# Splitting the first convolution load and moving the first low-rank second products in a two-layer convolution and low-rank FFN kernel

## What is computed

```
c0 = grouped_conv1d(x, weight, 9 taps, 4 groups) + cond @ c_weight.T + bias
x  = x + c0 @ W.T + b + mask * (c0 @ A.T) @ B.T          # low-rank adapters by batch entry
w  = softmax(mlp(cond));  c1 = (sum_k w_k W_k) @ x + sum_k w_k b_k
x  = x + 2 * sum_experts gate * (c1 @ A_e) @ B_e          # top 16 of 64 experts
```

## Time and profile before

| | |
|---|---|
| median of 3 runs | 661.34 us (660.93 to 661.41) |
| profiled execution | 659.91 us, its span 658.1 us |
| PE busy | 649.5 us (99% of the span) |
| VectorE, ScalarE, GpSimd busy | 451.2, 213.5, 72.9 us |
| memory traffic | 157.98 MB, 240 GB/s over the span |

### The profile page before, as it was taken

How to read it: one execution, slowest core, us unless ns; L and a number is a source line. 1 busy time by engine, 2 the same in 40 slices (tenths; PEclk the granted TensorE clock), 3 DMA queues, 4 the chain that set the end, 5 groups by cost and what they waited for, 6 DMA issues and landing times.

```text
span 658.1 us, 8354 instructions
## 1 busy us (share of the span) xinstructions
PE 649.5 (99%) x3197; PEld 537.6 (82%) x3197; DVE 451.2 (69%) x690; ACT 213.5 (32%) x275; POOL 72.9 (11%) x91
## 2 busy tenths in 40 slices
PE   9999999999999999999999999999999999999997
PEld 8878888888897788888789788888879888888875
DVE  2859469549378888558779648636867856665775
ACT  2714235315134024335124312334423421433420
POOL 1499300000000160000000042000000000000000
PEclk9999999999999999999999999999999999999999
DMA  8587714984988836776985682274987665037685
GB/s 314 196 292 279 296 49 135 356 247 167 392 280 346 336 149 255 272 225 251 366 296 186 266 319 96 101 225 161 366 323 268 259 252 190 0 116 206 223 333 215
DMA packets 51450, 157.98 MB, mean 240 GB/s; under 512 B 5472, under 2 KB 6368, under 8 KB 51424
## 3 DMA queue, kind: packets, MB, share of 16 engines
q1 hardware_dynamic: 46096, 148.05, 62.0%
q10 hardware_dynamic: 5328, 9.61, 4.8%
HBM read 131.94 MB, written 25.71 MB: 240 GB/s over the span
## 4 chain that ended last, share of the span: by engine, by line
PE 74%; DMA 12%; DVE 7%; issue 2%; ACT 2%; SPq 1%; ACTq 0%; DVEq 0%
PE bank L1367 19%; PE bank L1369 19%; PE bank L1368 19%; PE bank L1381 7%; DMA gate_x<-gates 5%; DMA piece_lo<-kept 4%; PE bank L1401 3%; DMA raw<-pieces 2%; PE bank L1388 2%; PE bank L1393 1%; PE bank L1407 1%; PE bank L1395 1%; DMA toep<-taps 1%; PE bank L1408 1%; DVE x L918 1%
## 5 line engine op out<-in xcount | busy, mean ns | idle before, releaser
L886 DVE TENSOR_TENSOR piece_lo<-raw,piece_hi 128x1024 fp32r<-128x1024 f32 x60 | 74.2, 1240 | 90.1 <-ACT piece_hi L639 89.8
L639 ACT ACTIVATE piece_hi<-raw 128x1024 fp32r<-128x1024 f32 x60 | 63.3, 1057 | 143.9 <-PE bank L1369 100.5
L1367 PE MATMUL bank<-piece_hi,u_hi 128*128 128x512 f32 x272 | 107.9, 397 | 0.1
L1369 PE MATMUL bank<-piece_hi,u_lo 128*128 128x512 f32 x272 | 107.3, 394 | 0.0
L1368 PE MATMUL bank<-piece_lo,u_hi 128*128 128x512 f32 x272 | 107.3, 394 | 0.0
L1367 PE MATMUL bank<-v_hi,piece_hi 128*128 128x512 f32 x256 | 101.8, 398 | 0.0
L1369 PE MATMUL bank<-v_hi,piece_lo 128*128 128x512 f32 x256 | 101.1, 395 | 0.0
L1368 PE MATMUL bank<-v_lo,piece_hi 128*128 128x512 f32 x256 | 101.0, 394 | 0.0
L1367 PE MATMUL bank<-piece_hi,v_hi 128*128 128x512 f32 x192 | 76.2, 397 | 1.1 <-DMA piece_lo<-kept 1.0
L1369 PE MATMUL bank<-piece_hi,v_lo 128*128 128x512 f32 x192 | 75.8, 395 | 0.0
L1368 PE MATMUL bank<-piece_lo,v_hi 128*128 128x512 f32 x192 | 75.8, 395 | 0.0
(11 more groups left out here) (143 smaller groups left out, 799.2 us busy)
## 6 DMA issues: line engine op xcount, KB each, us to landing
raw<-pieces SPq DMA_DIRECT2D x76, 512.0 KB, 5.3
piece_hi<-kept SPq DMA_DIRECT2D x48, 512.0 KB, 4.7
piece_lo<-kept SPq DMA_DIRECT2D x48, 512.0 KB, 6.1
conv_in<-conv_x SPq DMA_DIRECT2D x16, 516.0 KB, 6.8
x<-x SPq DMA_DIRECT2D x16, 512.0 KB, 5.4
gate_x<-gates ACTq DMA_DIRECT2D x32, 256.0 KB
out<-x SPq DMA_DIRECT2D x32, 256.0 KB, 4.4
conv_in<-pieces SPq DMA_DIRECT2D x12, 512.0 KB, 8.6
```

The source lines that it names most:

```text
L639: act.activation(piece_hi[:, n % SLOTS, :], raw[:, r % RAWS, :], ACT.Copy).then_inc(s_piece_hi, 1)
L886: dve.tensor_tensor(piece_lo[:, n % SLOTS, :], raw[:, r % RAWS, :], piece_hi[:, n % SLOTS, :].bitcast(F32), ALU.subtract).then_inc(s_piece ...
L1367: pe.matmul(to, left_hi, right_hi, start=first, stop=False)
L1369: return pe.matmul(to, left_lo, right_hi, start=False, stop=last)
```

## The change

The first load of convolution input brings entry 0 alone; entry 1's half follows behind taps 1 and taps 3, with a semaphore of its own, for which PE waits ahead of entry 1. In `ffn_piece`, the low-rank second products of the first half are issued behind all four tiles of piece 3, with their waits; those of the second half stay behind each tile of piece 7.

```diff
+        s_convin_b1 = sem("s_convin_b1")
...
-            load_conv_in(0, 0)
+            def load_first(b, done):
+                width = CG * (Q + 1)
+                sp.dma_start(conv_in[:, b].rearrange("p g q -> p (g q)"),
+                             conv_x[0, 0, :, b * width:(b + 1) * width]).then_inc(done, 16)
+
+            load_first(0, s_convin[0])
             load_taps(sp, 1)
             load_taps(sp, 3)
+            load_first(1, s_convin_b1)
             sp.dma_start(hidden_stage, hidden_w).then_inc(s_hidden_w, 16)
...
                         if t == NT - 1:
                             mm.then_inc(s_piece_used, 1)
-                        if j == 3:
-                            if t == 0:
-                                pe.wait_ge(s_lora_s, 2)
-                                pe.wait_ge(s_lora_lo, 1)
-                                if h == 0:
-                                    pe.wait_ge(s_const_hi, 3)
-                                    pe.wait_ge(s_const_lo, 2)
-                            lora_second(h, t, 4 * h + t, False)
+                        if n == 7:
+                            lora_second(1, t, 4 + t, False)
+                    if n == 3:
+                        pe.wait_ge(s_lora_s, 2)
+                        pe.wait_ge(s_lora_lo, 1)
+                        pe.wait_ge(s_const_hi, 3)
+                        pe.wait_ge(s_const_lo, 2)
+                        for t in range(NT):
+                            lora_second(0, t, t, False)
...
                     if b % 2 == 0:
                         pe.wait_ge(s_convin[b // 2], 16)
+                    elif b == 1:
+                        pe.wait_ge(s_convin_b1, 16)
```

## The result

| | before | after |
|---|---|---|
| median, 22 runs each | 660.51 us (658.61 to 662.91) | 658.83 us (657.23 to 661.17) |
| ratio after / before | | 0.9978, 95% interval 0.9968 to 0.9988 |
| profiled execution, its span | 659.91, 658.1 us | 658.74, 656.9 us |
| PE busy | 649.5 us | 649.5 us |

The ratio is 1.45 us of 660.51, with an interval from 0.8 to 2.1 us; the two medians are 1.68 us apart. The forecast of the difference, 1.5 us, was met.

The account below looks back on a forecast made before the run. TensorE (PE) was taken to set the pace, busy 649.5 of 658.1 us. The start's 0.35 us and the low-rank wait's 1.14 us sum to 1.49 us: 661.34 - 1.5 = 659.8 us, range 659.1 to 661.1.

Parts of the forecast that it names:

- The anchor: Starting time for the whole kernel: differences from the trace are subtracted from the runs' median of 661.34 us.
- Part 2: Low-rank second products behind all four tiles of piece 3: PE's wait there goes, 1.14 us, at least 0.9.
- the second copy: ScalarE copy before the low-rank second products: claimed to release PE at 48.51 us after 0.91 us without work.
- Part 1: Start of the kernel, first load halved: taps come earlier and PE starts 0.35 us sooner, bounds 0 and 0.45.
- the hidden weights: Weights of the first hidden product at the start: land at 8.32 us, against a use at 8.32, just in time.
- the wait of 0.42 us for taps: PE's wait before tap group 3 at the start, 0.23 to 0.42 us, taken as gone.
- Rival 1: Only the low-rank wait goes and the start stays as it is: 660.2 us, within 0.2%; chance 0.11.
- all engines are where they were, only earlier: From the second group's row-wise selection to the end, the chain moves by the same 1.5 us.
- The wait at 187.65 us: PE's first wait after 52 us, for VectorE, 0.47 us: appears near 186.2 with its size unchanged.
- 2: Rival: the second half's fixed cost is not overlapped, PE 1.25 us late on hidden weights: 661.4 us; chance 0.04.
- 3: Rival: the second half is stuck in the backlog, batch entry 1 is 4.2 us late: 664.4 us; chance 0.04.
- Rival 4: Gain taken back at the DMA-bound stretch, PE's wait at 187.65 us grows by 1 us: 660.9 us; chance 0.09.

Follow-up runs that it names:

- dose: Changed kernel with added products nobody reads: 24 gave ratio 1.0120 to the kernel before, 5 gave 1.0023 and 1.0030, 5 ahead of the mixing 1.0022.
- e11: Changed kernel with low-rank second products of tiles 0 and 1 behind tile 1, those of tiles 2 and 3 behind their own; ratio 0.9981 to the kernel before.
- e8: Changed kernel plus small fills by idle engines behind each tap group's landing; one execution, group 3 landed at 6.95 us.
- e7: Kernel before with the low-rank move alone, old load, plus small fills behind each tap group's landing; one execution, group 3 landed at 8.04 us.
- e2: Kernel before with only the low-rank second products moved, first load as before; ratio 0.9985 (0.9971 to 0.9999) to the kernel before.
- e6: The kernel before once more, unchanged; ratio 0.9999 (0.9984 to 1.0015).
- e1: Kernel before with only the first load split, low-rank products where they stood; ratio 1.0000 (0.9988 to 1.0013) to the kernel before.
- e12: The split load alone on the kernel before, a second time; ratio 1.0001 (0.9988 to 1.0013) to the kernel before.
- e10: The changed kernel once more, unchanged; ratio 0.9977 (0.9960 to 0.9993) to the kernel before.
- e16: The changed kernel a third time, unchanged; ratio 0.9982 (0.9970 to 0.9994) to the kernel before.
- e4: Changed kernel with 6 warm-up products in place of 12; median 660.75 us, ratio 1.0006 (0.9993 to 1.0019) to the kernel before.
- e3: Kernel before with 6 warm-up products in place of 12; median 661.93 us, ratio 1.0045 (1.0023 to 1.0066) to the kernel before.

## Why the prediction was right, and where it was not

**The anchor failed.** The step that put the time outside the range was "I take the differences from the trace and subtract them from the median", with 0.25 us for the spread of the runs. Three runs had given 661.34 us (660.93 to 661.41). 22 runs gave 660.51 us, from 658.61 to 662.91. The three lay 0.8 us above the median of the many, and their spread of 0.5 us stood for one of 4.3 us. Of the miss of 659.8 - 658.83 = 1.0 us, 0.8 is this, and the rest is 1.68 us between the medians in place of 1.5; no mechanism was wrong by as much. The range has a slip too: 659.7 less 0.25 is 659.45, and not 659.2.

**Part 2 was right in mechanism and size.** 1.14 us forecast, 1.16 measured in A, in the first profile after and in six more without a dose, always 35.35 us. One reading was wrong and cost nothing: it was VectorE's subtraction and not the second copy that released PE, and where that took 0.84 us the stall was 1.3 us, so that the close agreement is partly luck of the profile before. The waits moved behind 18 more products are covered with over 3 us to spare; e11 shows that six would do. GpSimd's start on the mixing weights was hidden as argued.

**Part 1 was right in mechanism and unproved in size.** The taps come sooner, group 3 by 0.36 us on average (1.08 in e8 against e7) where 0.58 was worked out, and the next late thing is the hidden weights, as the prediction put it, 8.4 us against 8.32. Over the eleven profiles with the split they landed at 8.25 to 8.85 us, so that they now and then held PE up themselves (0.20 us in e8). The first half is hidden by the warm-up. But the wait of 0.42 us for taps in the one profile was taken as the state of the kernel. It is one draw: in e2, with the old load, group 3 had landed at 7.49 us and the passes ran through with next to no wait (entry 1 at 8.63 us); in e6 the waits were longer (9.38). The 0.35 us is 0.24 us on average over 16 profiles, and by the times alone (e1, e12) anything from 0.9 us lost to 0.8 us gained. In the first profile after, the first weight piece started at 24.24 us where 23.9 was forecast and 24.26 measured before. Rival 1, that only the low-rank wait goes, cannot be told from the forecast by the whole kernel's time.

**The way to the end.** The prediction's 1:1 fits the change itself: 1.16 + 0.24 = 1.4 us against 1.45 (0.8 to 2.1) measured. The doses say that what is put in at 52 us can come out larger at the end. So the step "all engines are where they were, only earlier" is not a law of this kernel, and the good fit of the sum leaves room for both a smaller part 1 and a gain of more than 1:1. No single profile can decide it: from the mixing to PE's last product the twelve profiles without a dose took 574.3 to 576.4 us, whatever the kernel. That stays open. The wait at 187.65 us was taken for a fixed feature. It was missing in the first profile after, in e10 and in the unchanged kernel's second profile e6, and there again in e16 (0.3 and 0.4 us): it comes and goes without any change. It is also dearer than its rows. From the second group's first convolution to its first low-rank first product PE needs 25.43 us in the profile after, without the wait, and 26.67 in the one before, with waits of 0.47 and 0.23 us.

**The rivals.** 2 and 3 are refuted: the second half landed at 7.9 to 8.5 us in the profiles with the split, never behind the hidden weights, and its fixed cost was overlapped. The formula of the Trainium skill (DMA: Bandwidth & Descriptors, Anatomy of one DMA), which the page states for transfers issued by GpSimd, gives an estimate of 2.6 us for the half, and the trace shows 2.7 for this one, issued by SP. Adding a transfer to the busy queue did not add the fixed part to those behind: the hidden weights landed at 8.52 us on average with the split and at 8.40 with the old load. Rival 4, a gain taken back by transfers, did not occur in the median, though the waits for kept pieces differ by over 1 us from one profile to the next.

## What to carry to other kernels

A stall with a producer's chain behind it can be read from two starts in one profile, here to 0.02 us for that execution and to 0.15 us over several. Moving the waiting instructions behind independent work gave just that, and no more when they were moved further than the chain needs. The stall behind the transfers of the first microseconds was a draw here, different in each execution; look at such a stall in several executions before you give it a size. When the effect is a fifth of a per cent, the median of three runs is no anchor: forecast the difference, and give the time a range as wide as the runs of many executions.

## What was not expected of the hardware

- The time at which PE's passes begin to start 0.11 us apart instead of 0.21 us varied from 3.9 to 6.9 us over executions with the same twelve warm-up products. The granted clock from 2 to 8 us reads 1.00 all the while in the profile after, where the change came at 6.9.
- With six warm-up products PE waited nearly 2 us for taps in the profile of e4, and the granted clock fell to 0.50 from 8 to 14 us. In the profile of e3, with the old load, many passes still started 0.21 us apart up to 22.7 us, with the granted clock at 1.00, and the execution took 668.35 us. Both are the slowest executions of their kernels. Half a warm-up cost 3.0 us by the ratio of e3, while PE had been given work 1 us sooner.
- Five added products, 1.2 us of PE in the first group, cost 2.6 to 3.2 us at the end, with the excess in the second group. The kernel before comes to the mixing just as late, and its B is 133.2 us where theirs is 135.4 to 136.1.
- VectorE's subtraction for the low-rank products, the same instruction on the same shape, took 0.68 us in nine profiles and 0.83 to 0.87 in nine others, with GpSimd at another instruction beside it, and PE's stall followed it.
